# A decoder kernel in which the attended rows are turned, divided and turned back on VectorE in 32x32 blocks

## What is computed

```python
xn = layer_norm(x, ln1_w, ln1_b)
q, k, v = split(xn @ Wi.T + bi, 3)          # 16 heads of 16
out = softmax(q @ k.T / 4 + causal_and_distance) @ v
x = x + out @ Wo.T + bo                     # heads joined: 256
xn = layer_norm(x, ln2_w, ln2_b)
x = x + gelu(xn @ W1.T + b1) @ W2.T + b2
```

## Time and profile before

| | us |
|---|---|
| median of 3 runs | 3498.88 (3495.42 to 3504.38) |
| profiled execution | 3507.89, its span 3506.1 |
| decoder | about 0 to 1850 of the span |
| cross attention | about 1850 to 2190 |
| experts | about 2190 to 3506 |

### The profile page before, as it was taken

The page is one execution under the profiler, slowest core; times in us unless marked ns, Lnnn a source line. Parts: engine busy times, 40 slices in busy tenths (PEclk is TensorE's granted clock), DMA queues, the critical chain, the costliest instruction groups (busy, mean ns, idle before and its releaser), DMA issues. The chain is left out here.

```text
span 3506.1 us, 89278 instructions
## 1 busy us (share of the span) xinstructions
PE 3316.4 (95%) x36224; PEld 2280.0 (65%) x36224; DVE 2612.0 (74%) x5238; ACT 2305.6 (66%) x3540; POOL 1419.3 (40%) x1308
## 2 busy tenths in 40 slices
PE   5899999999999999999987888799999999999998
PEld 3567666676767666676664555466666666666665
DVE  4666667666666766666676888898888888888877
ACT  4677777767677776767754666566666566666665
POOL 1233232333323332332334543574444444445475
PEclk8999999999999999999997989899999999999999
DMA  3100111101111011100111122100000000000001
GB/s 123 42 29 29 41 50 37 38 29 41 41 46 35 26 39 50 46 29 29 35 43 54 58 67 68 62 13 27 13 15 27 1 26 1 27 1 27 1 13 37
DMA packets 104968, 124.49 MB, mean 36 GB/s; under 512 B 20240, under 2 KB 92560, under 8 KB 102416
## 3 DMA queue, kind: packets, MB, share of 16 engines
q1 hardware_dynamic: 104560, 118.78, 10.3%
HBM read 50.13 MB, written 8.39 MB: 17 GB/s over the span
## 5 line engine op out<-in xcount | busy, mean ns | idle before, releaser
L2814 POOL TENSOR_TENSOR e_hT<-e_h,e_hT 128x512 f16<-128x512 f32 x512 | 614.3, 1202 | 600.8 <-ACT e_hT L2563 577.6
L1202 DVE TENSOR_REDUCE mx<-maxima_pair 128x4 f16<-128x1024 f32 (+1 forms) x384 | 470.2, 1225 | 237.9 <-PE maxima_pair L681 235.1
L2557 ACT ACTIVATE e_h<-e_h,e_b 128x512 f32<-128x512 f32 x512 | 365.6, 714 | 416.3 <-DVE e_h L2643 416.3
L93 PE MATMUL bank<-xT,w_half 128*128 128x512 f16 x2400 | 564.9, 386 | 5.8 <-DVE xT L1145 4.0
L991 ACT ACTIVATE PR<-scores_pair 128x1024 f32<-128x1024 f32 x384 | 392.6, 1022 | 130.6 <-PE scores_pair L698 122.3
L1330 POOL TENSOR_TENSOR QK<-qk,QK 128x512 f16<-128x512 f32 x128 | 148.4, 1159 | 622.7 <-ACT qk L920 431.8
L93 PEld LDWEIGHTS bank<-xT,w_half 128*128 128x128 f16 x2400 | 227.0, 99 | 261.4 <-issue 21.3
L2501 PE MATMUL bank<-VS,e_hT 128*128 128x256 f16 x3072 | 389.0, 273 | 6.3 <-DVE VS L2606 4.6
L2501 PE MATMUL bank<-e_w,e_hT 128*128 128x256 f16 x3072 | 388.7, 273 | 4.5 <-POOL e_hT L2814 4.3
L2501 PEld LDWEIGHTS bank<-VS,e_hT 128*128 128x128 f16 x3072 | 300.3, 98 | 113.1 <-DVE VS L2606 5.1
L2501 PEld LDWEIGHTS bank<-e_w,e_hT 128*128 128x128 f16 x3072 | 300.6, 98 | 109.8 <-POOL e_hT L2814 6.5
(11 more groups left out here) (219 smaller groups left out, 6846.7 us busy)
## 6 DMA issues: line engine op xcount, KB each, us to landing
QS<-QK SPq DMA_DIRECT2D x240, 128.0 KB, 2.1
KS<-QK SPq DMA_DIRECT2D x192, 128.0 KB, 2.1
PR<-in_expert_weights SPq DMA_DIRECT2D x16, 1024.0 KB, 5.1
stage<-in_weights SPq DMA_DIRECT2D x48, 256.0 KB, 3.4
xT<-in_x SPq DMA_DIRECT2D x8, 512.0 KB, 3.6
xT_f<-xT SPq DMA_DIRECT2D x8, 512.0 KB, 3.7
stage<-xT_f SPq DMA_DIRECT2D x4, 1024.0 KB, 5.4
out<-stage SPq DMA_DIRECT2D x8, 512.0 KB, 3.3
```

The source lines that it names most:

```text
L93: last = pe.matmul(out, stat(a, k), mov(b, k), start=(k == 0 and n == 0), stop=(k == tiles - 1 and n == 2))
L1202: dve.tensor_reduce(out, src, AX.X, ALU.max, negate=True).then_inc(mx_in.sem, 1)
L2557: act.activation(h32[r % 2][:, j, :], h32[r % 2][:, j, :], ACT.Gelu, bias=b1[:, e, m:m + 1], scale=1.0 / WS)\
L2814: pool.tensor_tensor(hT[r % 2][1][:, f, part], h32[r % 2][:, j, :], hT[r % 2][0][:, f, part], ALU.subtract)\
```

## The change

In the decoder VectorE reads O. `turn_outputs(n, c)` is now a vector transpose of 128x512 f32, which turns each 32x32 block by itself, from O into `turned` (the old OTs), and signals `o_in`. `divide(n, c)` takes the reciprocals of the sums (one column of each block) and multiplies; the results of two steps stand side by side in `divided` (the old On). `join_outputs(n, k)` turns the blocks of two steps back with one more vector transpose. outputs_high and outputs_low read this from SBUF and add the value bias as a column per partition. The rows of the output weights are put in the matching order outside the kernel. Steps 0 to 2 are turned in the body of n, step 3 at the start of the next. TensorE's 16 and 8 transposes, the four copies on ScalarE and the two additions of the value bias on GpSimd go; `attend(n, 0)` waits for `v_f` in place of `v_in`. The list of tiles through the three PSUM banks is shorter by six.

The masking products of a score tile are shared: where each of two or four units had four products of 64 columns, there are now four products for all units, with the identity repeated (`unit_columns`) and an output that steps over the units (`diagonals`).

In the cross attention the value bias moves behind the division too; the transposes there stay on TensorE. One small DMA loads all value bias columns at the start.

```diff
-    mx, mrow, PR, OTs, On, oT = (shared[k] for k in ("mx", "mrow", "PR", "OTs", "On", "oT"))
-    rden = shared["rden"]
+    mx, mrow, PR, turned, oT = (shared[k] for k in ("mx", "mrow", "PR", "OTs", "oT"))
+    SQ = 32
+    BL = GT // SQ
+    rden = shared["rden"].rearrange("p c k -> p (c k)").rearrange("p (c k) -> p c k", c=C)
+    divided = shared["On"].rearrange("p t d -> p (t d)").rearrange("p (k n) -> p k n", k=KD)
+    assert C == 2 * KD and BL == H
 ...
-        out = f(("V", 0)) + b(("OS", 0, 1, 2, 3)) + f(("V", 1)) + b(("OT", 0)) + a(("T1", 0)) + b(("OT", 1))
+        out = f(("V", 0, 1)) + a(("T1", 0))
 ...
+        def diagonals(bank_pair, r, s, first, half):
+            blocks = bank_pair[:, r * GT:(r + 1) * GT]
+            if s < 2:
+                at = first + half * HALF
+                return blocks.rearrange("p (i k) -> p i k", i=2)[:, :, at:at + HALF]
+            return blocks.rearrange("p (x k) -> p x k", x=4)[:, :, half * HALF:(half + 1) * HALF]
+        def unit_columns(r, s):
+            times = 2 if s < 2 else 4
+            return ident_b[64 * r:64 * r + HALF, :].unsqueeze(1).to_broadcast([HALF, times, HALF])
 ...
                 q, keys, at = (b * T + P, T, i * T) if s < 2 else (b * T, P, i * T + b * P)
                 for r in range(2):
                     pe.matmul(M[:, r * GT + at:r * GT + at + keys], QS[64 * r:64 * r + R_MAX, 2 * c + i, q:q + P],
-                              KS[64 * r:64 * r + R_MAX, 2 * c + i, b * T:b * T + keys], start=True, stop=False)
-                for half in range(2):
-                    for r in range(2):
-                        to = r * GT + at + keys - P + half * HALF
-                        last = pe.matmul(M[:, to:to + HALF], mask_q[64 * r:64 * r + HALF, half, :],
-                                         ident_b[64 * r:64 * r + HALF, :], start=False, stop=half == 1)
+                              KS[64 * r:64 * r + R_MAX, 2 * c + i, b * T:b * T + keys], start=at == 0, stop=False)
+            for half in range(2):
+                for r in range(2):
+                    last = pe.matmul(diagonals(M, r, s, P, half), mask_q[64 * r:64 * r + HALF, half, :],
+                                     unit_columns(r, s), start=False, stop=half == 1)
             last.then_inc(M_ps.sem, 1)
 ...
-                pe.wait_ge(v_in.sem, v_in.after(n))
+                pe.wait_ge(v_f.sem, v_f.after(n))
             pe.wait_ge(p_in.sem, p_in.after(n, ST * (c + 1)))
             pe.wait_ge(o_in.sem, o_in.after(n, c))
 ...
@@ -769,28 +776,15 @@
                 key_scores(n, 0, 0)
                 row_scores(n, 2, 0)
                 values(kind, n, 0)
-            if back:
-                turn_outputs(kind, n, 0)
-                turn_outputs(kind, n, 1)
-            if front:
                 key_scores(n, 0, 1)
-            if back:
-                turn_outputs(kind, n, 2)
-                turn_outputs(kind, n, 3)
-            if front:
                 row_scores(n, 2, 1)
                 values(kind, n, 1)
-            if back:
-                pe.wait_ge(on_in.sem, on_in.after(n - 1))
-                turn(kind, n, "OT", 0, OT_ps, On)
             if ahead:
                 pe.wait_ge(z1.sem, z1.after(n + 1))
                 turn(kind, n, "T1", 0, T1_ps, z[0])
             if front:
                 key_scores(n, 0, 2)
                 row_scores(n, 2, 2)
-            if back:
-                turn(kind, n, "OT", 1, OT_ps, On)
 ...
-            act.wait_ge(OT_ps.sem, OT_ps.after(n - 1, k + 1))
+            act.wait_ge(joined.sem, joined.after(n - 1, k + 1))
             if k == 0:
                 act.wait_ge(OP_ps.sem, OP_ps.after(n - 2))
-            act.activation(oT[0][:, k, :], tile(kind, "OT", k)[:, :], ACT.Copy).then_inc(oh.sem, 1)
+            act.activation(oT[0][:, k, :], turned[:, 2 * k, :], ACT.Identity, bias=value_col(n - 1, k))\
+               .then_inc(oh.sem, 1)
 ...
-        def out_rows(n, c):
-            act.wait_ge(O_ps.sem, O_ps.after(n, c + 1))
-            if c == 0:
-                act.wait_ge(OS_ps.sem, OS_ps.after(n - 1))
-            act.activation(OTs[:, c, :], O[:, :], ACT.Copy).then_inc(o_in.sem, 1)
 ...
-        def outputs(kind, n, t):
-            dve.wait_ge(OS_ps.sem, OS_ps.after(n - 1, t + 1))
-            bank = tile(kind, "OS", t)[:, :].rearrange("p (h d) -> p h d", h=H)
-            if t == 0:
-                dve.wait_ge(OT_ps.sem, OT_ps.after(n - 2))
-            dve.reciprocal(rden[:, t, :], bank[:, :, HD]).then_inc(rd_in.sem, 1)
-            dve.wait_ge(rd_in.sem, rd_in.after(n - 1, t + 1))
-            dve.tensor_tensor(On[:, t, :].rearrange("p (h d) -> p h d", h=H), bank[:, :, 0:HD],
-                              rden[:, t, :].unsqueeze(2).to_broadcast([P, H, HD]), ALU.mult)\
+        def turn_outputs(n, c):
+            dve.wait_ge(O_ps.sem, O_ps.after(n, c + 1))
+            if c % 2 == 0:
+                dve.wait_ge(oh.sem, oh.after(n - 1, c // 2 + 1))
+                dve.wait_ge(ol.sem, ol.after(n - 1, c // 2 + 1))
+            dve.transpose(turned[:, c, :], O[:, :]).then_inc(o_in.sem, 1)
+        def divide(n, c):
+            blocks = turned[:, c, :].rearrange("p (b r) -> p b r", r=SQ)
+            dve.wait_ge(o_in.sem, o_in.after(n, c + 1))
+            dve.reciprocal(rden[:, c, :], blocks[:, :, HD]).then_inc(rd_in.sem, 1)
+            dve.wait_ge(rd_in.sem, rd_in.after(n, c + 1))
+            dve.wait_ge(joined.sem, joined.after(n - 1, c // 2 + 1))
+            to = divided[:, c // 2, :].rearrange("p (b r) -> p b r", r=SQ)[:, :, c % 2 * HD:(c % 2 + 1) * HD]
+            dve.tensor_tensor(to, blocks[:, :, 0:HD], rden[:, c, :].unsqueeze(2).to_broadcast([P, BL, HD]), ALU.mult)\
                .then_inc(on_in.sem, 1)
+        def join_outputs(n, k):
+            dve.wait_ge(on_in.sem, on_in.after(n, 2 * k + 2))
+            dve.transpose(turned[:, 2 * k, :], divided[:, k, :]).then_inc(joined.sem, 1)
 ...
-            dve.tensor_tensor(oT[1][:, k, :], tile(kind, "OT", k)[:, :], oT[0][:, k, :], ALU.subtract)\
-               .then_inc(ol.sem, 1)
+            dve.scalar_tensor_tensor(oT[1][:, k, :], turned[:, 2 * k, :], value_col(n - 1, k), oT[0][:, k, :],
+                                     ALU.add, ALU.subtract).then_inc(ol.sem, 1)
 ...
@@ -1218,10 +1217,9 @@
             if front:
                 maxima(n, 2, 0)
             if back:
-                outputs(kind, n, 0)
-                outputs(kind, n, 1)
-                outputs(kind, n, 2)
-                outputs(kind, n, 3)
+                turn_outputs(n - 1, 3)
+                divide(n - 1, 3)
+                join_outputs(n - 1, 1)
             if swap == 1:
                 weights(l, "qkv")
             if front:
@@ -1254,6 +1252,9 @@
             if back:
                 norm2_root(n, group(g, -1))
                 norm2_scaled(n, group(g, -1))
+            if front:
+                turn_outputs(n, 0)
+                divide(n, 0)
             if swap == 2:
                 weights(l, "o")
             if tail:
@@ -1262,6 +1263,10 @@
                 start.first_stats(dve, 2)
             if tail:
                 shrunk(kind, n, group(g, -2), 2)
+            if front:
+                turn_outputs(n, 1)
+                divide(n, 1)
+                join_outputs(n, 0)
             if ahead:
                 maxima(n + 1, 0, 0)
             if back:
@@ -1274,6 +1279,9 @@
                 maxima(n + 1, 0, 2)
             if tail:
                 shrunk(kind, n, group(g, -2), 3)
+            if front:
+                turn_outputs(n, 2)
+                divide(n, 2)
             if swap == 3:
                 weights(l, "f2")
             if ahead:
 ...
-        def values(n, k):
-            pool.wait_ge(v_f.sem, v_f.after(n, k + 1))
-            pool.tensor_tensor(VS[:, 2 * k:2 * k + 2, :, 0:HD], VS[:, 2 * k:2 * k + 2, :, 0:HD],
-                               rows[:, 0, :].rearrange("p (h d) -> p h d", h=H).unsqueeze(1)
-                               .to_broadcast([P, 2, H, HD]), ALU.add).then_inc(v_in.sem, 1)
 ...
-            act.activation(oT[0][:, k, :], work("OT", n, k)[:, :], ACT.Copy).then_inc(oh.sem, 1)
+            act.activation(oT[0][:, k, :], work("OT", n, k)[:, :], ACT.Identity, bias=value_col[k]).then_inc(oh.sem, 1)
 ...
-            dve.tensor_tensor(oT[1][:, k, :], work("OT", n, k)[:, :], oT[0][:, k, :], ALU.subtract)\
-               .then_inc(ol.sem, 1)
+            dve.scalar_tensor_tensor(oT[1][:, k, :], work("OT", n, k)[:, :], value_col[k], oT[0][:, k, :],
+                                     ALU.add, ALU.subtract).then_inc(ol.sem, 1)
 ...
+    turned = np.arange(D).reshape(KD, 2, C, HD).transpose(0, 2, 1, 3).reshape(D)
 ...
-        stationary(f["attn_out_proj_w"][l].T),
+        stationary(f["attn_out_proj_w"][l].T[turned]),
```

(48 more changed lines are left out.)

55 lines of the change are left out of this document (28 added, 27 removed).

## The result

| | before | after |
|---|---|---|
| median of 4 runs | 3501.63 us (3495.42 to 3572.62) | 3576.41 us (3573.34 to 3583.96) |
| ratio | | 1.0223, 95% interval 1.0203 to 1.0244 |
| profiled execution, and its span | 3507.89, 3506.1 | 3575.79, 3574.0 |
| mean granted clock of the profiled execution | 0.971 | 0.964 |

A forecast was written before the change was run, and what follows sets the result against it. TensorE, busy 95% of the span, was taken to bound the kernel. Ordinary bodies (23 x 2.4 us, 55), weight bodies (22) and the ends (-1) gave +76 us: 3584 profiled, 3575 as median, range 3480 to 3650.

The forecast's parts named there:

- transposes and masks off TensorE: Per decoder body, TensorE loses 16 transposes of OTs and 8 of On (3.2 us) and masking cost (0.15): 3.35 us.
- (a): Start of the body: TensorE waits 0.3 us for the exponential, 0.8 and 0.4 us for maxima, 1.5 us in sum.
- (b): attend(n,1) waits 2.7 us for bank O, which VectorE reads late in turn_outputs(n,0), behind norm2_scaled.
- (c): End of the body: transpose, division and join ahead of maxima(n+1,0,0) make row_scores(n+1,0,1) wait 0.2 us.
- clock: The wait of attend(n,1) is followed by a lower clock in 8 of 10 bodies at 1.7 us: +1.35 a body.
- The transpose: One VectorE transpose of 128x512 f32, six a body: bounds 0.6 and 1.2 us, taken as 0.65.
- rival 3: The f32 transpose takes 1.2 us and not 0.65: 2.7 us more a body, 3655 us; chance 0.15.
- The masks: Masking products: 256 a body become 96 at equal columns; bounds 0 and 0.3 us a body, taken as 0.15.
- Rival 1: The wait at attend(n,1) is there but the clock holds: some 3535 us; chance 0.13.
- The weight bodies: Six bodies splitting weights on VectorE at the start, where TensorE already waits: about +3.6 us each, 22 in all.
- Rival 2: VectorE reaches turn_outputs(n,0) in time: 3444 us, or 3400 without the waits at the start; chance 0.22.
- Rival 4: divide(n,0) is held until GpSimd's additions are through, turn_outputs(n,1) comes 1.0 us later: 3605 us; chance 0.07.

The follow-up runs named there:

- experiment 4: Changed kernel with the edits of experiment 1 and experiment 3, and division of step 1 and join of steps 0 and 1 behind maxima(n+1,0,0): 3433.71 us.
- experiment 5: On top of experiment 4, VectorE's splitting of new weights spread over the body and two hidden_low subtractions earlier: 3419.57 us, ratio to before 0.9746.
- experiment 6: The kernel before with the shared masking products alone; transposes, copies and bias stay as they were: 3495.33 us, ratio to before 0.9979.
- experiment 1: Changed kernel with turn_outputs(n,0) moved ahead of maxima(n,3,2) in VectorE's order: 3470.78 us, ratio to before 0.9907.
- experiment 2: Changed kernel with turn_outputs(n,0) done twice, the first time into a tile nobody reads: 3613.12 us, ratio to before 1.0315.
- experiment 7: The changed kernel with the masking products of the kernel before, 64 columns each: 3579.13 us, ratio to before 1.0215.
- experiment 3: Changed kernel with a small exponential ending ScalarE's body and, at body start, maxima and turn of step 3 between hidden_low subtractions, division and join later: 3545.07 us.
- experiment 8: The kernel before with only the decoder's value bias moved behind the division: 3501.61 us, ratio to before 0.9989.

## Why the prediction was right, point by point

The forecast held, at 3575 us against 3576.41, and by its main mechanism. Not all of its terms held. By body, with waits taken as the distance between starts that they add, against the same place where no wait stands (so attend(n,1) would have started at 806.04, 0.01 behind the product at 806.03 as elsewhere, and started at 808.84: 2.80 for an idle time of 2.58, for the end of the last matmul before a wait otherwise lies under the next one):

| step | predicted, us | measured, us | from |
|---|---|---|---|
| transposes and masks off TensorE | -3.35 | -3.68 | experiments 4 and 5 |
| (a) key_scores(n,0,1) | +0.3 | +0.87 | 784.47, [0.71] |
| (a) row_scores(n,2,1) | +0.8 | +0.37 | 785.18, [0.21] |
| (a) row_scores(n,2,2) | +0.4 | +0.48 | 788.41, [0.32] |
| (b) attend(n,1) | +2.7 | +2.80 | 808.84, [2.58] |
| (c) row_scores(n+1,0,1) | +0.2 | +0.28 | start at 817.26 and not 816.98 |
| body without the clock | +1.05 | +1.16 | 55.39 against 54.23 |
| clock | +1.35 | +0.8 | 14 of 28 waits, 1.57 each |

The measured terms ahead of the clock add up to +1.12, against +1.16 of the body itself, so no wait of size is missing in the list. Both sides of the sum were taken too low, the gain by 0.33 and the waits by 0.40, and the two errors cancel. Of the 3.68, 0.29 is the masks (experiment 6); so the transposes were worth some 3.4 us, where their rows gave 3.23 and I took 3.2.

**(b)** was right in place, cause and size, and experiments 1 and 2 show it from both sides: without it the body loses 2.58, with a longer transpose it gains what the transpose takes. Behind the removal the next wait is (c), which grows by 0.21, from 0.28 to 0.49; that is why the body got back 2.58 and not 2.80.

**(a)** was near in its sum (1.72 against 1.5) and wrong in its parts. The exponential of (0,0) doesn't start when the copies before it are through. ScalarE's timeline of the same body:

```profile
780.90 0.66 ACT L980 ACTIVATE spare<-bank,cols 128x512 f32<-128x512 f32 x1
782.10 1.28 ACT L987 ACT_TABLE_LOAD   x1 [0.53 <-PE scores_pair L714]
783.39 1.02 ACT L987 ACTIVATE PR<-scores_pair 128x1024 f32<-128x1024 f32 x1
```

The load of the exponential's table stands behind the wait for the scores, idle for 0.53, and starts only when they are there. Before, a copy of OTs stood in between; it ended at 703.05 in the body of the earlier trace rows, and the scores had been ready since 702.80, so this wait never showed: the earlier trace rows has the exponential but not why it starts there. I had moved it up by the copy's 0.60 and forgotten the load's own place. TensorE comes to row_scores(n,2,1) later for it, and finds mx 0.37 late and not 0.8.

**The transpose** was taken at 0.65 to 0.69, bounds 0.6 and 1.2. By the groups of the changed kernel it is 0.706 alone, some 0.63 from start to start:

```profile
L1140 DVE STREAM_TRANSPOSE OTs<-bank 128x512 f32<-128x512 f32 x128 | 90.3, 706 | 3.4 <-PE bank L738 3.4
```

The nearest row, one read of 512 elements, was the right guide, and rival 3 (1.2 us) falls. The Trainium skill (Vector Engine (DVE) Microarchitecture Reference, The reshape front-end and per-opcode configuration) says that the transpose sustains one element per cycle and lane; by that the trace agrees: in f32, too, the transpose takes about what the subtraction of that length takes here (0.63 against 0.60 us from start to start).

**The masks** gave 0.29 in experiment 6, not 0.15: the upper bound. The columns being the same, it is a cost per product: 160 products fewer, 1.8 ns each.

**The clock** is the term that was mis-sized most. Of 28 attends that waited 2.58 us, 14 were followed by the lower level, where I had taken 8 of 10; a fall cost 1.57 us, where I had taken 1.7. It is little more than half the price: 0.8 a body, not 1.35. Two bodies with the same wait, next to each other (busy PE, PEld, DVE, ACT, POOL; then the clock):

```profile
752.80:756.20 3.40, 3.40 (x32) 2.07 (x25) 0.42 (x2) 1.02 (x1) 3.40 (x6) 0.50 0.02 5
809.70:813.10 3.40, 3.40 (x46) 2.77 (x39) 0.47 (x2) 1.02 (x1) 3.40 (x5) 1.00 0.02 5
```

In the same 3.4 us TensorE starts 32 products at the lower level and 46 at the upper. Rival 1, that the clock holds, is half true in this way. What decides which wait is followed by a fall stays open: these two bodies are alike in their order and in the length of the wait. The traces show that the wait's length is not all. Of the 19 ordinary bodies among the 28, 7 had a fall, of the 9 bodies that load new weights 7. In experiment 7, with the same wait, it was 8 of 19 and 8 of 9. The bodies with new weights have other waits besides, and in experiment 3, with less idle time at the start, only 10 of 28 had a fall; that it is this other idle time that counts is my reading, which no run isolates. My "one ordinary body of four" ahead of experiment 2 was too low as well.

**The weight bodies** held: in a layer of eight bodies the one with new qkv weights cost +3.5 (60.77 to 64.26) where 3.6 was taken; that with new f1 weights and the one behind it +6.3 together (114.97 to 121.31) where 3.6 + 2.4 was; the other five cost +7.7 where 12 was taken, with one fall of the clock in them where four were taken (these lengths are from attend(n,0) to attend(n+1,0)). All of the miss is the clock's. In TensorE's timeline of a body with new f1 weights

```profile
1028.35 1.89 PE L93 MATMUL bank<-w_half,oT 128*128 128x256 f16 x12 [2.55 <-DVE oT L1177]
1045.87 0.69 PE L734 MATMUL bank<-PR,VS 128*32 128x256 f32 x8 [2.58 <-DVE OTs L1140]
1067.27 0.39 PE L694 MATMUL maxima_pair<-KS,QS 63*128 63x256 f16 x4 [2.28 <-DVE mx L1201]
```

the first is for outputs_low, which now stands behind transpose, division and join; before, TensorE waited 1.52 and 0.63 us at this place. The second is new. The third stood there before, at 2.27 us (VectorE splits weights).

**The sum.** From start to start the 30 bodies cost 63.4 us, where the prediction's terms gave 77. The decoder's first body and its tail cost +5, where -1 was taken, and the rest of the kernel -0.5. That is 68 between the profiled executions against 76: eight too many, 3575.8 where 3584 was forecast for such an execution. The median hides it, for the prediction took 9 off us because the profiled execution of before stood that far above its three runs. In the runs beside experiments 5 and 8 the median of before was 3505 us (17 runs), 3 below that execution, and that of after stands where its profiled execution does. So the forecast's closeness is luck: over 30 bodies the gain was taken 10 us too small, the waits 12 too small and the clock some 17 too large, the ends of the decoder 6 too small, and the offset of 9 went against what was left. That the kernel gets slower, and at which wait, is not luck.

**Rival 2** (faster) was false of this change, but the point at which it decides was right: with the wait gone, 3470.78. **Rival 4**, the division held by GpSimd, is true in the small. In the row at 809.01 above it takes 0.82 and not 0.42. GpSimd had begun its additions at 808.14:

```profile
808.14 5.70 POOL L1343 TENSOR_TENSOR x<-x,spare 128x256 f32<-128x256 f32 x8 [1.59 <-DVE z L160]
```

In nearly every body divide(n,0) takes this long, and the divisions of the other steps take 0.42. It got in between two of eight, and nothing waited for it. The Trainium skill (SBUF — State Buffer, Who interferes with whom) calls the ports that VectorE and GpSimd share an exclusive lock; a delay of 0.4 us, less than one addition (0.7), agrees with that.

## What to carry to other kernels

When a result is read out of a bank by another engine than before, the question is not how long the reading takes there, but where in that engine's order it stands, and who wants the bank next: here 0.7 us of work in the wrong place cost 2.6 us in each body, and moved by one line it turned a loss of 2.2% into a gain of 0.9%. Walk the new order on the timeline of one body before it is run, and reorder until the engine that bounds the kernel starts without a wait; only then is work taken off it worth its length. Each wait of this size also carries a chance of a lower clock behind it, so its removal gives more than it shows.

## What the runs showed of the hardware that was not expected

- A table load on ScalarE starts behind the semaphore wait of the activation that needs it: 782.10, idle 0.53 before it, and 1.28 long. A tiny activation of the same kind ahead of the wait takes it off the path; the wait of the scores fell from 0.71 to 0.28 us (experiment 3).
- The same idle stretch of 2.58 us on TensorE was followed by the half clock in 14 of 28 cases, at 1.57 us each. With 3.18 us (experiment 2) it was 21 of 28.
- The same wait was followed by the half clock more often in the bodies with new weights, which have longer waits besides: in 7 of 9 against 7 of 19 ordinary ones, and in 8 of 9 against 8 of 19 in experiment 7.
- An idle stretch on TensorE costs more than it shows, by 0.16 to 0.22 us each: the end of the last matmul before it is not covered by the next (0.87 between starts for 0.71 idle, 2.80 for 2.58).
- Of products with 64 columns, sharing made 160 fewer a body and gave 0.29 us with unchanged columns: 1.8 ns a product.
